# Splitting the pair matmuls of a recommendation tower into narrower tiles of the matrix array

## What is computed

```
e = stack([tbl_f[ids[:, f]] for f in range(40)], axis=1)      # 512 x 40 x 32
vi, vj = e[:, I], e[:, J]                                     # all 780 pairs i < j
z = einsum('bke,kef,bkf->bk', vi, W, vj)                      # W: 780 x 32 x 32
h = concatenate([z, dense_ctx], axis=1)                       # 512 x 796
h = maximum(h @ W_top1 + b_top1, 0)                           # 796 x 512
h = maximum(h @ W_top2 + b_top2, 0)                           # 512 x 256
y = h @ W_top3                                                # 512 x 1
```

## Time and profile before

| | us |
|---|---|
| median of 3 runs | 195.17 (194.7 to 195.27) |
| the profiled execution's own time | 194.21 |
| its span in the trace | 192.4 |
| PE busy | 177.0 (92%) |
| PE weight loads busy | 55.1 (29%) |
| DVE busy | 147.1 (76%) |
| ACT busy | 91.1 (47%) |
| POOL busy | 118.6 (62%) |

### The profile page before, as it was taken

How to read it: one execution, slowest core, us unless ns; L and a number is a source line. 1 busy time by engine, 2 the same in 40 slices (tenths; PEclk the granted TensorE clock), 3 DMA queues, 4 the chain that set the end, 5 groups by cost and what they waited for, 6 DMA issues and landing times.

```text
span 192.4 us, 3365 instructions
## 1 busy us (share of the span) xinstructions
PE 177.0 (92%) x1360; PEld 55.1 (29%) x1360; DVE 147.1 (76%) x141; ACT 91.1 (47%) x80; POOL 118.6 (62%) x106
## 2 busy tenths in 40 slices
PE   0799979994999999999999999999699999999994
PEld 0133333321333322322322223232122222223441
DVE  0779999887989978898789788987758868783500
ACT  3567999999899822443325405340132124210421
POOL 3877887787877877787777777887924022800000
PEclk9999999999999999999999999999999999999999
DMA  4999501000000187000000000000000000000000
GB/s 140 292 407 372 204 7 17 18 11 13 13 17 10 19 271 243 14 14 10 10 14 14 14 14 14 15 10 14 7 3 0 0 3 0 0 0 3 0 0 0
DMA packets 7191, 10.72 MB, mean 56 GB/s; under 512 B 2036, under 2 KB 4728, under 8 KB 7176
## 3 DMA queue, kind: packets, MB, share of 16 engines
q1 hardware_dynamic: 4104, 8.93, 13.0%
q0 software_dynamic: 3072, 1.58, 4.7%
HBM read 10.49 MB, written 0.00 MB: 55 GB/s over the span
## 4 chain that ended last, share of the span: by engine, by line
POOL 55%; PE 26%; issue 16%; DMA 1%; ACT 1%; DVE 0%; POOLq 0%; ACTq 0%
POOL rows L378 54%; PE z_ps L613 7%; PE ring_ps L596 7%; PE ring_ps L620 7%; PE ring_ps L656 4%; POOL prod L314 1%; DMA idx<-ids 1%; ACT copied L426 1%; ACT h L459 0%; PE ring_ps L583 0%; PE ring_ps L662 0%; DVE y_sb L523 0%; POOLq L314 0%; ACTq L425 0%
## 5 line engine op out<-in xcount | busy, mean ns | idle before, releaser
L378 POOL DMA_INDIRECT rows<-table,idx x96 | 104.2, 1085 | 31.4 <-issue 28.9
L314 DVE TENSOR_TENSOR prod<-ring_ps,emb 128x1024 f32<-128x1024 f32 x78 | 92.9, 1220 | 21.9 <-PE ring_ps L596 21.7
L596 PE MATMUL ring_ps<-emb,wall 32*128 32x512 f32 (+1 forms) x400 | 62.2, 639 | 4.2 <-DVE prod L314 1.5
L613 PE MATMUL z_ps<-prod,consts_sb 128*32 128x512 f32 x400 | 50.0, 600 | 1.6 <-POOL prod L314 1.6
L426 ACT ACTIVATE copied<-ring_ps 128x1024 f32<-128x1024 f32 x22 | 22.5, 1025 | 56.7 <-PE ring_ps L596 56.7
L596 PEld LDWEIGHTS ring_ps<-emb,wall 32*128 32x128 f32 (+1 forms) x400 | 17.2, 183 | 43.3 <-DVE prod L314 21.7
L620 PE MATMUL ring_ps<-zt,w_sb 128*128 128x512 f32 x56 | 27.2, 615 | 0.0
L314 POOL TENSOR_TENSOR prod<-copied,emb 128x1024 f32<-128x1024 f32 x6 | 14.1, 2366 | 18.6 <-ACT copied L426 18.5
L402 ACT ACTIVATE distance<-ids,vocab 128x2048 f16<-128x2048 f16 x11 | 22.0, 2000 | 3.3 <-PE ring_ps L570 2.7
L405 ACT ACTIVATE one_hot<-distance,vocab 128x2048 bf16<-128x2048 f16 x11 | 22.0, 2002 | 0.4
L481 DVE TENSOR_SCALAR one_hot<-ids,vocab 128x2048 bf16<-128x2048 f16 x25 | 18.3, 771 | 2.3 <-PE ring_ps L570 1.5
(11 more groups left out here) (25 smaller groups left out, 56.6 us busy)
## 6 DMA issues: line engine op xcount, KB each, us to landing
w_sb<-w SPq DMA_DIRECT2D x1, 1792.0 KB, 8.1
rows<-table,idx POOLq DMA_INDIRECT x96, 2.4
table<-hot_table SPq DMA_DIRECT2D x2, 640.0 KB, 5.0
table<-hot_table SPq DMA_DIRECT2D x2, 512.0 KB, 4.2
wall<-w_pairs SPq DMA_DIRECT2D x1, 640.0 KB, 9.8
wall<-w_pairs SPq DMA_DIRECT2D x1, 576.0 KB
wall<-w_pairs SPq DMA_DIRECT2D x1, 512.0 KB, 8.3
w_sb<-w SPq DMA_DIRECT2D x1, 512.0 KB, 9.2
```

Source lines behind the costliest of these rows:

```text
L314: return eng.tensor_tensor(prod[:, o % RING_P], products, emb[:, slots:slots + 1, :].to_broadcast([P, 2, BATCH]), ALU.mult)
L378: nc.gpsimd.indirect_dma_start(rows[:, k, c, r, :], None, tables[f], bass.IndirectOffsetOnAxis(ap=idx[:, c, f:f + 1], axis=0)).then_inc(ga ...
L596: mm = nc.tensor.matmul(pair(("map", g), i // 2)[:, i % 2, :], wall[own, g, :], emb[own, stream, :], start=True, stop=True)
L613: mm = nc.tensor.matmul(z_ps[DIM * g:DIM * (g + 1), :], sel[:, m, :], prod[:, t // 2 % RING_P, t % 2, :], start=m == 0, stop=last)
```

## The change

In `map_group` each matmul of 128 columns becomes two of 64 columns. The first takes the columns 0 to 63 of the same weight block and writes the partitions 0 to 63 of the same bank, the second the columns 64 to 127 and the partitions 64 to 127. Both read the same rows of `emb`. So a group of two different quads is eight matmuls of 32 rows by 64 columns, which are eight different tiles of the array, and a quad with itself is four of 64 by 64. The signals stay where they were, now on the second matmul of the pair. Nothing else changes.

```diff
--- before.py
+++ after.py
@@ -593,8 +593,10 @@
                 height = P // 2 if slots == stream else DIM
                 for i in range(P // height):
                     own = slice(height * i, height * (i + 1))
-                    mm = nc.tensor.matmul(pair(("map", g), i // 2)[:, i % 2, :], wall[own, g, :], emb[own, stream, :],
-                                          start=True, stop=True)
+                    for c in range(2):
+                        half = slice(P // 2 * c, P // 2 * (c + 1))
+                        mm = nc.tensor.matmul(pair(("map", g), i // 2)[half, i % 2, :], wall[own, g, half],
+                                              emb[own, stream, :], start=True, stop=True)
                     if i % 2:
                         mm.then_inc(mapped, 1)
```

## The result

| | before | after |
|---|---|---|
| median of 20 runs each, same chip, us | 194.73 (193.89 to 195.62) | 194.11 (193.05 to 194.82) |
| ratio, 95% interval | | 0.9965 (0.9948 to 0.9982) |
| the profiled execution's span, us | 192.4 | 191.5 |
| PE busy, us | 177.0 | 175.3 |
| PE weight loads busy, us | 55.1 | 50.5 |

The change is faster by 0.35% (0.18 to 0.52%), 0.7 us (0.62 us between the medians), where 0.36 us and "no difference that can be told" were forecast. The time lies just inside the range, at its low end. The ratios in this document leave out executions that took over 1.5% more than the fastest of the same kernel: none here, and further down one of the kernel before (200.65 us), four of e7 and one each of e8, e9 (350.9 us) and e10 (197.29 us).

The account below looks back on a forecast made before the run. GpSimd's gathers and product were taken to bound the kernel until 138.69 us, TensorE afterwards. There 11 x 0.025 + 2 x 0.04 = 0.36 us gained, from 195.17 to 194.8 us; range 194.1 to 195.7 us.

Parts of the forecast that it names:

- The price of a group: Each TensorE group: shorter load less longer tile lag, 0.022 to 0.025 us gained; a quad with itself 0.036 to 0.04.
- the lag of eight tiles 7 ns apart: Group's end: the last of eight tiles starts 49 ns after the first instead of 21, costing 0.028 us a group.
- The passes: TensorE groups: 512 streamed columns still take 0.43 us a pass if all eight tiles run at once; costed at nothing.
- rival 1: Slower: two tiles of one row strip don't run side by side; about 238 us, mild form 196.4 us; chance 0.07.
- The switch of form: Before and behind nearly every group: changing form still costs 0.09 us without the lag.
- rival 3: Faster: the switch between groups and sums costs less, 2.3 us more gain, 192.5 us; chance 0.05.
- the line: Weight loads at 0.8 ns a column between 32 and 128 columns; puts the exposed 64-column load at 0.05 us.
- rival 4: A 64-column load takes as long as 128, leaving only the lag: 195.5 us, 0.2% slower; chance 0.12.
- The last stretch: TensorE from 138.69 to 175.7 us, 11 groups of 8 and 2 of 4: forecast to gain 0.36 us.
- what TensorE gains before 138.69 us only lengthens this wait: Sum at 138.69 us waits 1.6 us for GpSimd's product; earlier gains only lengthen that to about 2.7 us.
- The 1.1 us of the head: TensorE's 42 earlier groups gain some 1.1 us, all given back to the wait for GpSimd.
- Rival 2: Faster: the gain before 138.69 us counts too, as gathers are held up or the wait is partly something else; 193.6 us; chance 0.06.

Follow-up runs that it names:

- e7: Kernel before (whole matmuls) with op 68's product moved from GpSimd to VectorE: 195.13 us, ratio to the kernel before 0.9978.
- e8: The change (split matmuls) with op 68's product moved from GpSimd to VectorE: 194.41 us, ratio to the kernel before 0.9934.
- e9: Kernel before with op 68's product on VectorE and twelve matmuls of zeros in TensorE's two pauses: 193.41 us, ratio 0.9931.
- e10: The change with op 68's product on VectorE and twelve matmuls of zeros in TensorE's two pauses: 192.48 us, ratio to the kernel before 0.9879.
- e11: Kernel before with twelve matmuls of zeros, a quarter of GpSimd's gathers replaced by plain transfers (values differ from the reference): 192.36 us, ratio 0.9895.
- e12: The change with twelve matmuls of zeros, a quarter of GpSimd's gathers replaced by plain transfers: 191.37 us, ratio to the kernel before 0.9831.
- e5: Kernel before with twelve matmuls of zeros in TensorE's two pauses between 42 and 47 us: 193.96 us, ratio 0.9958.
- e14: Kernel before, unchanged, run for a second extra trace; the clock fell (mean 0.991): 193.98 us.
- e2: Matmuls split only in the first 42 groups, the others whole as in the kernel before: 194.45 us, ratio 0.9984.
- e1: Matmuls split only in the last 13 groups, the others whole as in the kernel before: 194.39 us, ratio 1.0004.
- e6: The change with twelve matmuls of zeros in TensorE's two pauses between 42 and 47 us: 193.59 us, ratio to the kernel before 0.9944.
- e16: Kernel before with groups of two quads as sixteen tiles of 32 by 32, plus twelve matmuls of zeros: 194.89 us, ratio 0.9997.

## Why the prediction was wrong

**What held.** The price of a group: 0.05 us less for the load, 0.028 more for the lag of eight tiles 7 ns apart, 1.04 us where 1.04 to 1.05 was worked out; a quad with itself 1.02. From the group at 47.30 us on, e11 and e12 show the same price over the whole program. The passes kept their 0.43 us, so rival 1 fell: the eight tiles of a group, two to a strip of rows, run side by side. The switch of form kept its 0.08 to 0.09 us (second pass 0.56, less 0.43 and 0.05 of lag, against 0.54 - 0.43 - 0.02), so rival 3 fell, and the load of 64 columns was no longer than the line says, so rival 4 fell. The last stretch gained 0.32 to 0.33 us of the 0.36 forecast; the rest is the wait for ScalarE's copy (0.04 us), which the sum had left as it was.

The rule of the Trainium skill (TensorE: Matmul & The Clock Gate, Part 3) that a weight load overlaps running matmuls only where the row group differs is contradicted once more: the 16 loads of a group, of both passes, fill 0.23 us together (151.51 in the trace after), before the second pass starts at 151.99, while matmuls of the same rows run, and the group lasts 1.04 us, where turns would have made it 1.9. In the same part, under "The mechanism", the Trainium skill also lets a load into a background weight buffer go ahead of running matmuls; which way these loads took, no run here tells.

**The step that failed** is the first one: "what TensorE gains before 138.69 us only lengthens this wait". It was read from one execution, in which TensorE was 1.6 us early. That was the kind with the clock at 2.4 GHz throughout, 30 of the 99 executions of the kernel before. In 39 of them the clock falls to 1.2 GHz in the pauses at 42 to 48 us for some 7 us, TensorE loses more than those 1.6 us (the sum starts at 139.5 to 139.8 us where TensorE stood ready near 137.1), and the sum waits for TensorE. The 1.1 us of the head, costed at nothing, then count in part: 0.85 us in the traces. Even at full clock the wait at 138 us did not grow to 2.7 as forecast: it was 1.7, and the earlier wait for gathered rows took the rest. Nor is the wait a fixed cover there: in e5's trace, whose gathers end at 135.1 us, it is 0.3 us. The wait of 1.6 us was the cover of that term, and I had not asked what takes it away; the three runs of the kernel before, 0.5 to 1.1 us above the profiled execution, were a sign that I passed over as a difference to carry along (their clock is not on record). How the 0.7 us of the first measurement divide between the tail, the head and the shares of the levels cannot be told: over all executions of the table the means of the two kernels differ by 0.56 us. Rival 2 had the right outcome (the head counts too) with another mechanism, and too small a chance. That the time lies inside the range is in part luck: the forecast of 194.8 us was built on a median of three executions, 195.17 us, and twenty gave the kernel before 194.73.

**The scatter** of both kernels, 1.7 to 1.8 us between the extremes, goes with the same two things: the fall of the clock, and the end of the gathers, which lay between 135.0 and 136.8 us in the traces of before and after. What moves the gathers is not settled. Nor is why the gain at a mean clock of 0.99 is 0.2 us and not the 1 us that e14's trace and the head's price would give; the gathers ended later in e2's trace (136.6) than in e14's (135.0), which would take the gain away, but that is two traces.

## What to carry to other kernels

Narrower tiles of the array buy exactly the exposed part of a weight load (0.8 ns a column, behind each switch of form) and pay 7 ns for every further tile at the next switch; eight tiles win 0.03 us a group here, sixteen nothing. Before a gain is costed at nothing because it ends in a wait, compare the profiled execution's time with the median and its mean clock with that of the others: if the others are slower, the wait may not be there in them. Short pauses of TensorE in the middle of a kernel can cost on top of what they last: here 0.5 and 1.4 us by the level in the kernel before (193.94 us against 194.47 and 195.31), and 2.1 and 2.9 us with op 68 on VectorE, where nothing covers the loss. Zeros multiplied into a bank that is being accumulated are a cheap filling: e5 takes 193.90 us in the mean, as the kernel before at full clock.

## What was not expected of the hardware

- With two pauses (busy 3.1 of 6 us from 42 to 48 us) the granted clock fell to 1.2 GHz in about two of three executions, for some 3.4 or 7 us, and in the others not at all, with the same program and nearly the same times. The small differences may decide: in the eleven traces without zeros and with all gathers the group between the pauses starts at 43.92, 44.11 and 44.41 us where the clock stayed (e1, after, before) and at 44.55 to 45.31 us where it fell (the other eight). Why is open.
- Twelve matmuls of zeros in these pauses kept it from falling in all 24 executions of e5 and e6, so matmuls with no data but zeros hold it up. Of the 40 executions of the later kernels with zeros (e9 to e12, e16) one, of e10, had a mean clock of 0.953.
- Behind a group of sixteen tiles (32 loads and 32 matmuls within 1.07 us) the next step takes longer (two sums 1.87 us against 1.85); behind eight tiles it doesn't.
